# Four graph layers on one core: interleaved bn_stats without merging, probability copies on VectorE, and new orders of work

## The chip, the cores and the metric

The kernel runs on one core of a Trainium2 chip. Its time is the device time in microseconds, from one launch, median of three runs. In the core, TensorE (PE), VectorE (DVE), ScalarE (ACT), GpSimd (POOL) and SyncE (SP) each work through their own list of instructions and wait for each other by semaphores. Here SP issues all transfers of the steady state.

## The reference

128 graphs of 128 nodes with 256 features pass through four residual layers over one adjacency matrix. Each begins with a layer norm and a ReLU:

```
def _layernorm(x, axis=-1, eps=1e-05):
    m = jnp.mean(x, axis=axis, keepdims=True)
    v = jnp.var(x, axis=axis, keepdims=True)
    return (x - m) / jnp.sqrt(v + eps)
...
    h = jnp.maximum(_layernorm(x, axis=-1), 0.0)
    x = x + _L0_gnn_ref(h, adj, L0_gnn_W, L0_gnn_a)        # graph attention, 128 features, and the features themselves
    h = jnp.maximum(_layernorm(x, axis=-1), 0.0)
    x = x + _L1_gnn_ref(h, adj, L1_gnn_W, L1_gnn_b)        # deg * (x Wi + b) + A (x Wj)
    h = jnp.maximum(_layernorm(x, axis=-1), 0.0)
    x = x + _L2_gnn_ref(h, adj, ...)                       # masked attention, 8 heads of 32
    h = jnp.maximum(_layernorm(x, axis=-1), 0.0)
    x = x + _L3_gnn_ref(h, adj, L3_gnn_W, L3_gnn_a_src, L3_gnn_a_dst)   # graph attention, 256 features
```

## The kernel before

Two graphs (GROUP = 2) make a group, and 64 groups pass through a pipeline of eight parts, 0 to 7. Every engine has a function `slot` that lists its pieces in a fixed order, each with its part: `at(5, split_head_3)` does that piece for group t - 5. `run` calls `slot` for t = 0 to 70 (64 groups and PARTS = 7). One pass over the list is called a slot in this text. The order inside a slot is written out by hand for each engine, and a piece waits by semaphore for the piece that feeds it and for the one that frees its PSUM bank.

The eight PSUM banks of 512 fp32 columns are shared by name: `f0_ps`, `sc0_ps` and so on each point to a bank. x of a group lies as `[128 nodes, 2 graphs, 256]` in fp32, in one of 11 buffers.

A layer goes like this. VectorE takes the statistics of x, one bn_stats for each graph (six numbers: count, mean and summed squares of the even and of the odd elements), and one bn_aggr for each graph merges them to mean and variance. GpSimd makes the scale and shift from them (`add_eps`, `negate_mean`, `power`, `shift`). ScalarE applies them with the ReLU (`norm0_0`, `norm0_1`, one for each graph). GpSimd splits the result into a high and a low fp16 part (`rows_hi`, `rows_lo`), SP transposes both by DMA (`move0` to `move3`), and TensorE multiplies by weights that are split in the same way, three matmuls for one product (`triple`). The two attention layers with one head (0 and 3) turn the probabilities on TensorE (`turn_probs0`, `turn_probs3`). ScalarE copies them from PSUM to SBUF (`keep_probs0`, `keep_probs3`), TensorE sums with them (`gat_sum0`, `gat_sum3`) and VectorE adds the result to x (`update0_0`, `update3_0` and their partners). The head attention keeps its probabilities in PSUM, casts them on ScalarE (`keep_head`), subtracts on VectorE (`split_head`) and turns both parts by DMA (`move_heads_hi`, `move_heads_lo`).

A slot has on TensorE: 90 matmuls of 256 or 258 columns (84 of the weights' triples, four for biases, two for masks), 12 of 130 columns, 48 of 33 columns, two of 512 for the gather, four fp32 ones each of 256 and 129 columns as recorded, eight small fp32 ones of 128, and the head scores. On SP it has one load of x, seven transposes and one store.

Of the kernel before, what the change touches and what calls it, by code (L numbers as in the profile page):

```python
# [21 lines left out]
FOLD = [0, 1, 2, 3]  # L22
# [20 lines left out]
def build(nc, x_in, adj, adj_t, w0, w0_t, a0, w_i, w_j, b1, w_q, w_k, b_qk, w_v, b_v, w_o, b_o, w3, w3_t, a3, out):  # L43
# [7 lines left out]
    with ctx:  # L51
# [42 lines left out]
        stats0 = pair("stats0", [P, GROUP, 6], F32)  # L94
        moments0 = pair("moments0", [P, GROUP, 2], F32)
        vareps0, rstd0, nmean0, nshift0 = (pair(n, [P, GROUP], F32) for n in ("vareps0", "rstd0", "nmean0", "nshift0"))
        relu0 = pair("relu0", [P, GROUP, D], F32)
        stats1 = pair("stats1", [P, GROUP, 6], F32)
        moments1 = pair("moments1", [P, GROUP, 2], F32)
        vareps1, rstd1, nmean1, nshift1 = (pair(n, [P, GROUP], F32) for n in ("vareps1", "rstd1", "nmean1", "nshift1"))  # L100
        relu1 = pair("relu1", [P, GROUP, D], F32)
        stats2 = pair("stats2", [P, GROUP, 6], F32)
        moments2 = pair("moments2", [P, GROUP, 2], F32)
        vareps2, rstd2, nmean2, nshift2 = (pair(n, [P, GROUP], F32) for n in ("vareps2", "rstd2", "nmean2", "nshift2"))
        relu2 = pair("relu2", [P, GROUP, D], F32)
        stats3 = pair("stats3", [P, GROUP, 6], F32)
        moments3 = pair("moments3", [P, GROUP, 2], F32)
# [45 lines left out]
        f0_ps = ps[6]  # L153
        r0_ps = ps[6]
        p0_ps = ps[0]
        s0_ps = ps[0]
        mj_ps = ps[5]
        mi_ps = ps[2]
        ag_ps = ps[5]
        q_ps = ps[0]  # L160
        k_ps = ps[4]
        v_ps = ps[5]
        sc0_ps = ps[7]
        sc1_ps = ps[4]
        sc2_ps = ps[1]
        sc3_ps = ps[3]
        sh0_ps = ps[0]
        sh1_ps = ps[2]
        pr_ps = ps[2]
        f30_ps = ps[7]  # L170
        f31_ps = ps[3]
        r3_ps = ps[5]
        p3_ps = ps[6]
        s3_ps = ps[6]
# [16 lines left out]
        stats0_0_done = sem("stats0_0_done")  # L191
# [4 lines left out]
        norm0_1_done = sem("norm0_1_done")  # L196
# [14 lines left out]
        update0_0_done = sem("update0_0_done")  # L211
        update0_1_done = sem("update0_1_done")
        add_feat0_done = sem("add_feat0_done")
        stats1_1_done = sem("stats1_1_done")
# [6 lines left out]
        relu_lo1_done = sem("relu_lo1_done")  # L221
        move1_done = [sem(f"move1_done_{k}") for k in range(2)]
# [7 lines left out]
        stats2_1_done = sem("stats2_1_done")  # L230
# [4 lines left out]
        norm2_0_done = sem("norm2_0_done")  # L235
# [7 lines left out]
        split_query_done = sem("split_query_done")  # L243
# [5 lines left out]
        head_max_0_done = sem("head_max_0_done")  # L249
        head_exp_0_done = sem("head_exp_0_done")  # L250
        head_max_1_done = sem("head_max_1_done")
# [4 lines left out]
        keep_head_0_done = sem("keep_head_0_done")  # L256
# [4 lines left out]
        split_head_2_done = sem("split_head_2_done")  # L261
# [17 lines left out]
        stats3_1_done = sem("stats3_1_done")  # L279
# [12 lines left out]
        leaky3_0_done = sem("leaky3_0_done")  # L292
# [3 lines left out]
        inv_sum3_done = sem("inv_sum3_done")  # L296
# [3 lines left out]
        update3_1_done = sem("update3_1_done")  # L300
# [12 lines left out]
        def _(sp):  # L313
# [51 lines left out]
            def move_heads_lo(g):  # L365
                sp.wait_ge(split_head_2_done, g + 1)
                sp.dma_start(head_t_lo[g % 2][:, :, :], head_lo[g % 2][:, :, :].rearrange("p a n -> p (a n)"), transpose=True).then_inc(move_heads_lo_done[g % 2], 16)
# [9 lines left out]
            def store_x(g):  # L377
                sp.wait_ge(update3_1_done, g + 1)
                sp.dma_start(out_groups[g], x[g % XBUF][:, :, :]).then_inc(x_moved[g % XBUF], 16)

            def slot(at):
                at(0, load_x)
                at(7, move3)
                at(6, move_out)
                at(2, move1)
                at(5, move_heads_hi)
                at(5, move_heads_lo)
                at(0, move0)
# [8 lines left out]
        def _(pe):  # L397
# [41 lines left out]
            def feat0(g):  # L439
# [3 lines left out]
                if g >= 7:  # L443
                    pe.wait_ge(update3_1_done, g - 6)
# [6 lines left out]
            def logit_rows0(g):  # L451
                if g == 0:
                    pe.wait_ge(mask_ready, 1)
                pe.wait_ge(keep_feat0_done, g + 1)
                logit_rows(r0_ps, g0[g % 2], 130).then_inc(logit_rows0_done, 1)

            def turn_probs0_0(g):
                pe.wait_ge(expo0_0_done, g + 1)
                if g >= 3:
                    pe.wait_ge(split_query_done, g - 2)  # L460
# [12 lines left out]
            def message_source(g):  # L473
# [3 lines left out]
                if g >= 5:  # L477
                    pe.wait_ge(leaky3_0_done, g - 4)
# [6 lines left out]
            def message_own(g):  # L485
                if g == 0:
                    pe.wait_ge(w_split, W_TURN.index("i") + 1)
                if g >= 4:
                    pe.wait_ge(update2_done, g - 3)
# [12 lines left out]
            def make_query(g):  # L502
# [4 lines left out]
                if g >= 2:  # L507
                    pe.wait_ge(split_out_0_done, g - 1)
# [9 lines left out]
            def make_key(g):  # L518
                if g == 0:
                    pe.wait_ge(w_split, W_TURN.index("k") + 1)  # L520
                if g >= 1:
                    pe.wait_ge(split_head_1_done, g)
# [433 lines left out]
        def _(act):  # L956
# [16 lines left out]
            def norm0_1(g):  # L973
# [4 lines left out]
                if g == 0:  # L978
                    hi_part("i", COL_WI, D)
# [359 lines left out]
```

## Time and profile before

| | us |
|---|---|
| median of three runs | 1150.78 (1149.5 to 1151.24) |
| time of the profiled execution | 1155.16 |
| its span, first to last instruction | 1153.4 |
| PE busy | 1067.4 (93%) |
| DVE busy | 1045.6 (91%) |
| ACT busy | 1057.2 (92%) |
| POOL busy | 950.6 (82%) |

The mean granted TensorE clock is 0.978 of full speed. Busy time is the time in which at least one instruction of an engine is shown. Instructions overlap in it, since the next one starts before the last has written its result, so what an instruction costs its engine is the distance from its start to the next start where nothing is waited for. The shares hold the fill and the drain of the pipeline too; between them all four engines are busier.

### The profile page before, as it was taken

Reading aid. Unit: us, or ns where it says so; the run is one execution under the profiler, and the core shown is the slowest. Engines: PE = TensorE matmul, PEld = TensorE weight load, DVE = VectorE, ACT = ScalarE, POOL = GpSimd, SP = SyncE. Lnnn points to the kernel's source line nnn. Section 1 sums busy time; section 2 is a strip of 40 time slices with the busy share of each in tenths; the row PEclk is TensorE's granted clock in tenths of the full one; section 3 lists DMA queues with packets and bytes.
Section 4 is the critical chain, followed back from the end, with each engine's and each line's share of the span. In section 5 each row is a group of like instructions: output and inputs, shape, how many; then the busy total and the mean of one; then the engine's idle time right before and its main releaser. Section 6 shows DMA issues by size and latency. Waiting matters only on the chain.

```text
span 1153.4 us, 38860 instructions
## 1 busy us (share of the span) xinstructions
PE 1067.4 (93%) x14872; PEld 881.4 (76%) x14872; DVE 1045.6 (91%) x2911; ACT 1057.2 (92%) x3145; POOL 950.6 (82%) x1734
## 2 busy tenths in 40 slices
PE   4589999999999999999999999999999999999864
PEld 3467888888888878788878878887888888888642
DVE  4469999999999999999999999999999999999861
ACT  3479999999999999999999999999999999999852
POOL 3778998998988889898989889888988899898421
PEclk9889999999999999999999999999999999999985
DMA  5369999999999999999999999999999999999861
GB/s 148 65 110 147 180 175 172 187 184 172 175 184 175 164 177 182 170 183 172 175 180 174 177 182 171 172 184 184 167 175 184 178 182 168 183 179 156 140 121 40
DMA packets 643515, 190.07 MB, mean 165 GB/s; under 512 B 607232, under 2 KB 643328, under 8 KB 643328
## 3 DMA queue, kind: packets, MB, share of 16 engines
q1 hardware_dynamic: 642560, 187.24, 93.6%
q8 instruction: 118, 1.93, 0.7%
q14 instruction: 69, 0.57, 0.2%
q10 hardware_dynamic: 768, 0.33, 0.1%
HBM read 19.73 MB, written 16.78 MB: 32 GB/s over the span
## 4 chain that ended last, share of the span: by engine, by line
ACT 32%; DVE 32%; DMA 16%; PE 11%; issue 3%; POOL 3%; SPq 1%; DVEq 0%; POOLq 0%
DMA x<-in_x 9%; DMA h_t<-h_rows 5%; DMA mix_t<-mix_rows 3%; PE ps L406 3%; PE ps L408 2%; PE ps L407 2%; DVE x L787 2%; DVE head_nmax L826 2%; ACT ps L1060 2%; DVE head_nmax L822 2%; DVE x L878 2%; ACT ps L1055 2%; ACT ps L1049 2%; ACT ps L1066 2%; ACT relu L971 1%
## 5 line engine op out<-in xcount | busy, mean ns | idle before, releaser
L406 PE MATMUL ps<-w_hi,h_t 128*128 128x256 f16 (+2 forms) x1280 | 328.3, 266 | 31.1 <-DMA h_t<-h_rows 21.5
L407 PE MATMUL ps<-w_lo,h_t 128*128 128x256 f16 (+2 forms) x1280 | 329.9, 265 | 0.0
L408 PE MATMUL ps<-w_hi,h_t 128*128 128x256 f16 (+2 forms) x1280 | 329.7, 265 | 0.0
L406 PEld LDWEIGHTS ps<-w_hi,h_t 128*128 128x128 f16 x1280 | 125.4, 98 | 59.3 <-DMA h_t<-h_rows 26.9
L408 PE MATMUL ps<-h_t,w_lo 128*128 128x256 f16 x512 | 139.6, 273 | 0.0
L407 PE MATMUL ps<-h_t,w_hi 128*128 128x256 f16 x512 | 139.6, 273 | 0.0
L406 PE MATMUL ps<-h_t,w_hi 128*128 128x256 f16 x512 | 139.6, 273 | 0.0
L408 PEld LDWEIGHTS ps<-w_hi,h_t 128*128 128x128 f16 x1280 | 125.8, 98 | 14.3
L407 PEld LDWEIGHTS ps<-w_lo,h_t 128*128 128x128 f16 x1280 | 126.5, 99 | 12.4
L406 PEld LDWEIGHTS ps<-v_hi,head_t_hi 128*128 128x128 f16 x1024 | 82.5, 96 | 13.5 <-issue 4.2
L406 PE MATMUL ps<-v_hi,head_t_hi 128*128 128x33 f16 x1024 | 90.4, 178 | 1.3 <-issue 1.2
L407 PEld LDWEIGHTS ps<-v_lo,head_t_hi 128*128 128x128 f16 x1024 | 80.1, 96 | 13.5 <-issue 0.6
L408 PE MATMUL ps<-v_hi,head_t_lo 128*128 128x33 f16 x1024 | 90.4, 178 | 0.0
L407 PE MATMUL ps<-v_lo,head_t_hi 128*128 128x33 f16 x1024 | 90.3, 178 | 0.0
L1227 POOL TENSOR_TENSOR x<-x,deg_b 128x512 f32<-128x512 f32 x64 | 81.7, 1276 | 0.0
L1247 POOL TENSOR_TENSOR x<-x,out_bias 128x512 f32<-128x512 f32 x64 | 81.2, 1269 | 0.0
L408 PEld LDWEIGHTS ps<-v_hi,head_t_lo 128*128 128x128 f16 x1024 | 79.9, 96 | 0.0
L1222 POOL TENSOR_TENSOR h_rows<-relu,h_rows 128x512 f16<-128x512 f32 x64 | 73.9, 1155 | 5.3
L1060 ACT ACTIVATE ps<-ps,head_nmax 128x128 f32<-128x128 f32 x256 | 77.3, 448 | 0.0
L1278 POOL TENSOR_TENSOR h_rows<-relu,h_rows 128x512 f16<-128x512 f32 x64 | 74.3, 1161 | 0.4
L1255 POOL TENSOR_TENSOR h_rows<-relu,h_rows 128x512 f16<-128x512 f32 x64 | 74.1, 1158 | 0.3
L1195 POOL TENSOR_TENSOR h_rows<-relu,h_rows 128x512 f16<-128x512 f32 x64 | 74.0, 1157 | 0.3
(181 smaller groups left out, 4445.4 us busy)
## 6 DMA issues: line engine op xcount, KB each, us to landing
x<-in_x SPq DMA_DIRECT2D x64, 256.0 KB, 3.3
out<-x SPq DMA_DIRECT2D x64, 256.0 KB, 2.6
h_t<-h_rows SPq DMA_TRANSPOSE x256, 3.8
head_t_hi<-head_hi SPq DMA_TRANSPOSE x64, 4.5
head_t_lo<-head_lo SPq DMA_TRANSPOSE x64, 6.1
mix_t<-mix_rows SPq DMA_TRANSPOSE x64, 3.5
w_f<-in_w_o SPq DMA_DIRECT2D x1, 256.0 KB, 3.8
w3t_f<-in_w_t SPq DMA_DIRECT2D x1, 256.0 KB, 3.8
```

The lines of the kernel that those rows point to most:

```text
L406: pe.matmul(o, lh, rh, start=start, stop=False)
L407: pe.matmul(o, lh, rl, start=False, stop=False)
L408: return pe.matmul(o, ll, rh, start=False, stop=stop)
L787: dve.scalar_tensor_tensor(x[g % XBUF][:, :, :], mi_ps[:, :].rearrange("p (b n) -> p b n", b=GROUP), deg_unscale[:, 0:1], x[g % XBUF][:, : ...
L822: dve.tensor_reduce(head_nmax[g % 2][:, 0, :], sc0_ps[:, :].rearrange("p (j n) -> p j n", n=P), AX.X, ALU.max, negate=True).then_inc(head_ ...
L1060: last = act.activation(sc2_ps[:, j * P:(j + 1) * P], sc2_ps[:, j * P:(j + 1) * P], ACT.Exp, bias=head_nmax[g % 2][:, 2, j:j + 1])
L1195: pool.tensor_tensor(h0_rows[g % 2][:, 1, :, :], relu0[g % 2][:, :, :], h0_rows[g % 2][:, 0, :, :], ALU.subtract).then_inc(rows_lo0_done, 1)
L1222: pool.tensor_tensor(h1_rows[g % 2][:, 1, :, :], relu1[g % 2][:, :, :], h1_rows[g % 2][:, 0, :, :], ALU.subtract).then_inc(relu_lo1_done, 1)
L1227: pool.tensor_tensor(x[g % XBUF][:, :, :], x[g % XBUF][:, :, :], deg_b1[:, :].unsqueeze(1).to_broadcast([P, GROUP, D]), ALU.add)
L1247: pool.tensor_tensor(x[g % XBUF][:, :, :], x[g % XBUF][:, :, :], out_bias[:, :].unsqueeze(1).to_broadcast([P, GROUP, D]), ALU.add)
L1255: pool.tensor_tensor(h2_rows[g % 2][:, 1, :, :], relu2[g % 2][:, :, :], h2_rows[g % 2][:, 0, :, :], ALU.subtract).then_inc(rows_lo2_done, 1)
L1278: pool.tensor_tensor(h3_rows[g % 2][:, 1, :, :], relu3[g % 2][:, :, :], h3_rows[g % 2][:, 0, :, :], ALU.subtract).then_inc(rows_lo3_done, 1)
```

## The change

Three things are changed. First, each layer takes the statistics of both graphs by one bn_stats over 512 elements: the access pattern `p b n -> p n b` makes graph 0 the even and graph 1 the odd elements, so that the six numbers are count, mean and summed squares of the one and the other. The bn_aggr go, and GpSimd takes the mean at index 1 and the sum at index 2, which it scales by 1/256. Second, `keep_probs0` and `keep_probs3` move from ScalarE to VectorE. Third, every engine has a new order of its slot, PSUM banks are dealt out anew, and semaphores follow both. The number of parts, of buffers and of transfers is as it was.

```
-            def stats3_0(g):
+            def mean_var3(g):
                 dve.wait_ge(update2_done, g + 1)
-                dve.bn_stats(stats3[g % 2][:, 0, :], x[g % XBUF][:, 0, :])
-
-            def stats3_1(g):
-                dve.bn_stats(stats3[g % 2][:, 1, :], x[g % XBUF][:, 1, :]).then_inc(stats3_1_done, 1)
-
-            def mean_var3(g):
-                dve.wait_ge(stats3_1_done, g + 1)
-                dve.bn_aggr(moments3[g % 2][:, 0, :], stats3[g % 2][:, 0, :])
-                dve.bn_aggr(moments3[g % 2][:, 1, :], stats3[g % 2][:, 1, :]).then_inc(mean_var3_done, 1)
+                dve.bn_stats(stats3[g % 2][:, :, :].rearrange("p b s -> p (b s)"), x[g % XBUF][:, :, :].rearrange("p b n -> p n b")).then_inc(mean_var3_done, 1)
...
-                pool.tensor_scalar(vareps3[g % 2][:, :], moments3[g % 2][:, :, 1], 1.0, EPS, ALU.mult, ALU.add).then_inc(add_eps3_done, 1)
+                pool.tensor_scalar(vareps3[g % 2][:, :], stats3[g % 2][:, :, 2], 1.0 / D, EPS, ALU.mult, ALU.add).then_inc(add_eps3_done, 1)
...
-            def keep_probs3(g):
-                act.wait_ge(turn_probs3_1_done, g + 1)
-                act.activation(prob_t3[g % 2][:, :], p3_ps[:, 0:GROUP * P], ACT.Copy).then_inc(keep_probs3_done, 1)
...
+            def keep_probs3(g):
+                dve.wait_ge(turn_probs3_1_done, g + 1)
+                dve.tensor_copy(prob_t3[g % 2][:, :], p3_ps[:, 0:GROUP * P]).then_inc(keep_probs3_done, 1)
```

The other three layers' statistics and `keep_probs0` change alike. SP's new order:

```
                 at(0, load_x)
+                at(1, move0)
                 at(7, move3)
                 at(6, move_out)
-                at(2, move1)
                 at(5, move_heads_hi)
                 at(5, move_heads_lo)
-                at(0, move0)
+                at(2, move1)
                 at(3, move2)
                 at(7, store_x)
```

The new orders of the other engines, in short form (part, piece), as they stand after the change:

```
vector: 2 mean_var1, 6 head_norm_1, 5 split_head_3, 5 head_max_2, 6 split_out_0, 3 split_message, 6 split_out_1,
  3 update1_own, 0 mean_var0, 3 update1, 3 mean_var2, 5 split_head_1, 5 split_head_2, 5 split_head_0,
  4 split_query, 4 split_key, 1 row_max0, 6 update2, 6 mean_var3, 7 row_max3, 4 head_max_0, 1 keep_probs0,
  4 head_max_1, 7 inv_sum3, 7 keep_probs3, 4 head_max_3, 4 split_value, 1 inv_sum0, 7 update3_1, 7 update3_0,
  1 update0_0, 5 invert_heads_0, 1 update0_1, 5 head_norm_0, 5 invert_heads_1
scalar: 3 norm2_0, 3 norm2_1, 1 expo0_0, 1 expo0_1, 7 leaky3_0, 7 leaky3_1, 0 norm0_1, 7 expo3_0, 7 expo3_1,
  0 norm0_0, 4 keep_value, 6 norm3_0, 6 norm3_1, 4 head_exp_3, 4 head_exp_1, 4 keep_head_3, 5 keep_out_0,
  4 head_exp_0, 2 keep_message, 5 keep_out_1, 4 keep_head_1, 4 head_exp_2, 4 keep_head_0, 4 keep_head_2,
  0 keep_feat0, 1 norm1_1, 1 norm1_0, 3 cast_query, 0 leaky0_1, 3 cast_key, 6 keep_feat3_1, 0 leaky0_0,
  6 keep_feat3_0
tensor: 1 turn_probs0_1, 4 make_value, 7 turn_probs3_0, 7 turn_probs3_1, 1 gat_sum0, 7 gat_sum3, 5 head_sum_0,
  5 head_sum_1, 2 message_source, 2 message_own, 3 make_query, 2 gather, 0 feat0, 3 make_key, 0 logit_rows0,
  6 feat3_1, 6 feat3_0, 5 project_0, 5 project_1, 6 logit_rows3, 3 head_scores, 0 turn_probs0_0
```

## Rows read from the trace of the kernel before

**Rows 1.** The page, part 1: busy time, share of the span and instructions.

```profile
PE 1067.4 (93%) x14872; PEld 881.4 (76%) x14872; DVE 1045.6 (91%) x2911; ACT 1057.2 (92%) x3145; POOL 950.6 (82%) x1734
```

**Rows 2.** Windows, steady stretch: busy time (instructions), clock, DMA share, GB/s.

```profile
200.00:1000.00 800.00, 781.55 (x11230) 653.10 (x11227) 777.36 (x2179) 790.90 (x2373) 716.61 (x1303) 1.00 1.02 177
```

**Rows 3.** Timeline, DVE, one slot: start, length, engine, line, operation.

```profile
599.38 0.68 DVE L829 TENSOR_REDUCE head_nmax<-ps 128x4 f32<-128x512 f32 x1
...
601.56 0.68 DVE L840 TENSOR_TENSOR head_lo<-ps,head_hi 128x512 f16<-128x512 f32 x1
603.05 0.43 DVE L729 BATCH_NORM_STATS2 stats<-x 128x6 f32<-128x256 f32 x1 [0.80 <-DMA x<-in_x]
...
603.72 0.41 DVE L801 BATCH_NORM_STATS2 stats<-x 128x6 f32<-128x256 f32 x1
604.04 0.17 DVE L733 BATCH_NORM_AGGREGATE moments<-stats 128x2 f32<-128x6 f32 x1
...
604.33 0.39 DVE L742 TENSOR_REDUCE nmax<-leaky 128x2 f32<-128x256 f32 x1
...
616.27 0.68 DVE L829 TENSOR_REDUCE head_nmax<-ps 128x4 f32<-128x512 f32 x1
```

**Rows 4.** Timeline, ACT, the same slot.

```profile
603.47 0.77 ACT L1036 ACTIVATE query_hi<-ps 128x512 f16<-128x512 f32 x1
604.75 0.40 ACT L998 ACTIVATE prob<-leaky,nmax 128x128 f32<-128x128 f32 x1 [0.51 <-DVE nmax L742]
...
608.39 0.38 ACT L1007 ACTIVATE prob_t<-ps 128x256 f32<-128x256 f32 x1
608.65 0.61 ACT L1032 ACTIVATE relu<-x,nshift,rstd 128x256 f32<-128x256 f32 x1
```

**Rows 5.** Timeline, PE, around the sum of layer 3.

```profile
612.66 0.27 PE L408 MATMUL ps<-w_hi,h_t 128*128 128x256 f16 x1
612.77 1.03 PE L636 MATMUL ps<-g,prob_t 128*128 128x256 f32 x4
613.64 0.18 PE L406 MATMUL ps<-v_hi,head_t_hi 128*128 128x33 f16 x1
613.67 0.18 PE L407 MATMUL ps<-v_lo,head_t_hi 128*128 128x33 f16 x1
```

**Rows 6.** Waits from 200 to 1000: total us, times, longest.

```profile
DVE stats L729 <- DMA x<-in_x: 12.2, 19, 1.2
```

**Rows 7.** Timeline, DVE: neighbours that wait for nothing but each other.

```profile
607.02 0.68 DVE L814 SCALAR_TENSOR_TENSOR key_lo<-ps,key_hi 128x512 f16<-128x512 f32 x1
607.62 0.68 DVE L878 SCALAR_TENSOR_TENSOR x<-ps,x 128x512 f32<-128x512 f32 x1
608.34 0.43 DVE L882 BATCH_NORM_STATS2 stats<-x 128x6 f32<-128x256 f32 x1
...
616.87 0.41 DVE L870 TENSOR_TENSOR mix_rows<-ps,mix_rows 128x256 f16<-128x256 f32 x1
617.20 0.41 DVE L874 TENSOR_TENSOR mix_rows<-ps,mix_rows 128x256 f16<-128x256 f32 x1
```

**Rows 8.** Timeline, SP and DVE: last update, load of x, first statistics.

```profile
614.56 0.43 DVE L907 SCALAR_TENSOR_TENSOR x<-ps,inv,x 128x256 f32<-128x256 f32 x1
...
615.46 0.48 SPq L318 DMA_DIRECT2D x<-in_x  x1
...
619.05 0.41 DVE L729 BATCH_NORM_STATS2 stats<-x 128x6 f32<-128x256 f32 x1
```

**Rows 9.** Timeline, all engines, the last group in the drain.

```profile
1144.88 0.36 ACT L1108 ACTIVATE leaky<-ps,g 128x128 f32<-128x128 f32 x1
1145.27 0.42 DVE L894 TENSOR_REDUCE nmax<-leaky 128x2 f32<-128x256 f32 x1 [8.51 <-ACT leaky L1108]
1145.73 0.40 ACT L1116 ACTIVATE prob<-leaky,nmax 128x128 f32<-128x128 f32 x1 [0.49 <-DVE nmax L894]
...
1147.17 0.38 ACT L1125 ACTIVATE prob_t<-ps 128x256 f32<-128x256 f32 x1 [0.56 <-PE ps L631]
```

More of the change, by code:

```diff
@@ L910, in slot @@
             def slot(at):
-                at(6, head_norm_0)
+                at(2, mean_var1)
                 at(6, head_norm_1)
+                at(5, split_head_3)
                 at(5, head_max_2)
                 at(6, split_out_0)
+                at(3, split_message)
                 at(6, split_out_1)
-                at(3, stats2_0)
-                at(5, split_head_3)
+                at(3, update1_own)
+                at(0, mean_var0)
+                at(3, update1)
+                at(3, mean_var2)
@@ L932, in slot @@
-                at(6, stats3_1)
+                at(6, mean_var3)
                 at(7, row_max3)
-                at(6, mean_var3)
+                at(4, head_max_0)
+                at(1, keep_probs0)
                 at(4, head_max_1)
+                at(7, inv_sum3)
+                at(7, keep_probs3)
+                at(4, head_max_3)
+                at(4, split_value)
                 at(1, inv_sum0)
-                at(4, head_max_3)
+                at(7, update3_1)
+                at(7, update3_0)
@@ L938, in slot @@
                 at(1, update0_0)
-                at(7, inv_sum3)
+                at(5, invert_heads_0)
                 at(1, update0_1)
-                at(1, stats1_0)
-                at(1, stats1_1)
-                at(4, head_max_0)
-                at(1, mean_var1)
-                at(2, split_message)
-                at(2, update1_own)
-                at(7, update3_0)
-                at(5, invert_heads_0)
-                at(7, update3_1)
-                at(2, update1)
+                at(5, head_norm_0)
@@ L979, in norm0_1 @@
                     hi_part("i", COL_WI, D)
+            def norm0_1(g):
+                act.wait_ge(shift0_done, g + 1)
+                act.activation(relu0[g % 2][:, 1, :], x[g % XBUF][:, 1, :], ACT.Relu, bias=nshift0[g % 2][:, 1:2], scale=rstd0[g % 2][:, 1:2])
             def keep_feat0(g):
@@ L1160, in slot @@
+                at(5, keep_out_0)
+                at(4, head_exp_0)
                 at(2, keep_message)
-                at(7, keep_probs3)
-                at(6, norm3_0)
+                at(5, keep_out_1)
+                at(4, keep_head_1)
+                at(4, head_exp_2)
+                at(4, keep_head_0)
+                at(4, keep_head_2)
+                at(0, keep_feat0)
+                at(1, norm1_1)
+                at(1, norm1_0)
+                at(3, cast_query)
+                at(0, leaky0_1)
```

354 lines of the change are left out of this document (149 added, 205 removed).

## The prediction

> **What bounds the kernel now.** I read the windows first. In the 800 us from 200 to 1000, tensor, vector and scalar are busy 781.55, 777.36 and 790.90 us, GpSimd 716.61 [rows 2]. Vector runs 45 instructions per group (2911 in all, about 30 of them for the setup) [rows 1], so the 2179 of that stretch are 48.4 slots, and a slot takes 800 / 48.4 = 16.52 us. Nobody is far from full; the question is who is full by need and who by waiting.
>
> For that the timeline of one vector slot is read by the distance from one start to the next, since the durations overlap (0.68 us for an operation that is followed after 0.60). From `head_max_3` to `head_max_3` it is 616.27 - 599.38 = 16.89 us. `split_head_1` at 601.56 is followed only at 603.05 by the statistics that wait for x, 1.49 us in place of 0.60: 0.89 us of waiting [rows 3]. Some 0.1 us more stands before `head_max_1`. What is left, **15.9 us, is vector's work per slot**. On scalar the same is done at the step from `cast_query` to `expo0_0`: 604.75 - 603.47 = 1.28 us where 0.48 would do, and little elsewhere, so **scalar's work is about 15.95 us** of those 16.89 [rows 4]. (The number is my estimate: 16.89 less 0.80 less about 0.1.)
>
> Tensor looks 97.7% busy, but a matmul that is shown for 0.27 us is followed after 0.11, a fp32 one of 256 columns after about 0.22, one of 33 columns after 0.025 [rows 5]. Each break in the stream therefore adds a tail that costs nothing. By these spacings I estimate a slot's work: 90 matmuls of 256 columns or about that 9.9 us, 12 of 130 columns 0.7, 48 of 33 columns 1.2, the fp32 sums and turns 2.2, the gather 0.4, the head scores about 1.1, together 15.4 us. GpSimd: 716.61 / 48.4 = 14.8.
>
> So two engines with 15.9 us each, in a slot of 16.52: 0.6 us is lost as they wait for each other, for x and for tensor. The chain of waits over the same stretch names x as the largest of vector's: 12.2 us, 0.25 per slot [rows 6].
>
> **The change, part by part.**
>
> *Statistics.* Removed per slot: eight bn_stats over 256 elements and eight bn_aggr. Two of the first take 603.72 - 603.05 = 0.67 us, so 0.33 each, 2.65 for eight. The last of three starts at 603.72 and the first merge at 604.04; four merges fill 604.04 to 604.33, 0.07 each, 0.58 for eight with the two that stand behind another operation at 0.09 [rows 3]. That is 3.23 us off vector. Added: four bn_stats over 512 elements, which alternate between the two graphs' rows, 1 KB apart. No row reads SBUF in such steps. If the stream runs at full rate, the price is that of 256 more elements on 0.33: operations over 512 elements follow each other after 0.60 [rows 7], so 0.33 + 0.27 = 0.60, and four cost 2.40. That is the lower bound. The upper bound is every element read at half rate: 0.60 + 0.53 = 1.13, four cost 4.52. I take 0.60, because it is what the vector operation of 512 elements costs in these rows, and bn_stats over 256 lies on the same line as the others of 256 (0.33).
>
> The Trainium skill speaks against this in one place: "Advanced Engine Details and Errata", section "Memory Cachelines", says that an access to a different 16-byte line each time pays a penalty. Its "Vector Engine (DVE) Microarchitecture Reference", section 5.2, gives 1.73 ns per column for a two-source operation of which one source hops at every element, yet says that a one-source operation alternating between two regions was measured at full rate. No run here shows either. By 1.73 ns the operation would cost an estimated 0.95 us, vector 17.2 us per slot, and the kernel about 1205 us.
>
> *A new neighbour.* `mean_var2` now stands right behind `update1`, whose result it reads. Where that is so today, `update2` before the statistics, the step is 608.34 - 607.62 = 0.72 instead of 0.60 [rows 7]: plus 0.11.
>
> *Copies of turned probabilities.* `keep_probs0` and `keep_probs3` leave scalar. `keep_probs0` is followed after 608.65 - 608.39 = 0.26 us [rows 4]; two of them are 0.53 off. On vector an operation of 256 columns from PSUM costs 617.20 - 616.87 = 0.33 [rows 7], two 0.66 more.
>
> *Sum.* Vector 15.9 - 3.23 + 2.40 + 0.11 + 0.66 = 15.84 us. Scalar 15.95 - 0.53 = 15.42. Tensor 15.4 and GpSimd 14.8 as before; the smaller inputs of `add_eps` and the scale 1/D cost nothing new. So vector alone bounds the slot, and its own work hardly shrinks: the gain has to come from waiting, 0.6 us today.
>
> *The orders.* On SP, the load of x stands behind the store as before; today the store's releaser `update3_1` starts at 614.56, the load is issued at 615.46 and its reader starts at 619.05, 4.5 us behind 614.56 [rows 8]. In the new order vector starts `update3_0` with about 1.4 us left in the slot (that operation, `update0_0`, `invert_heads_0`, `update0_1`, `head_norm_0`, `invert_heads_1`), and `mean_var0` comes after eight operations, 4.0 us: 5.4 us. 0.9 us more room covers the wait of 0.25. Moving `move0` behind the load and `move1` behind the two head moves changes when SP issues, not how often; the number of transposes (seven per slot) and the depth (PARTS, 7) stay, so I book the fill and drain at zero. With scalar 0.4 us below vector, its results should more often lie ready.
>
> I therefore take the wait from 0.6 to 0.3 us: slot 15.84 + 0.3 = 16.14, that is 0.38 less than 16.52; over 64 slots 24 us. Against the profiled span of 1153.4 (its own time was 1155.16) this is 1129; against the median of the runs, 1150.78, it is **1127 us**.
>
> **Rivals.**
>
> *Waits stay (1145).* Vector and tensor are then the pair that gets in each other's way, the DMA share stays at 1.02 [rows 2], and 0.6 us remain: 15.84 + 0.6 = 16.44, 0.08 x 64 = 5 us, 1145. For it: three engines within 0.5 us. Against it: the largest wait, for x, has a cause that the order removes.
>
> *The interleaved read is slow (1200).* It decides from where vector's work passes 16.52 less the 0.3 of waits, 16.22: 0.38 us over my sum, or 0.70 us per operation instead of 0.60. At the upper bound of 1.13 vector has 15.84 + 2.12 = 17.96, with 0.1 of waits (all others have slack) 18.06, 1.54 x 64 = 99 us, 1250. The middle between 1151 and 1250 is 1200. For it: a stream whose every element lies elsewhere is nowhere in the trace. Against it: the output is six numbers, and only one source is read.
>
> *The softmax of the last layer runs out of room on vector (1165).* The chain goes from `row_max3` over scalar and tensor to `keep_probs3`, now vector's, and on to `gat_sum3` and `update3_1`, in one slot. In the drain, where nobody else interferes, the first half takes 1147.17 - 1145.27 = 1.90 us [rows 9]; the new order leaves vector 0.32 + 0.60 + 0.33 + 0.60 + 0.07 = 1.92. The second half needs 0.38 for the copy, 1.03 for four matmuls [rows 5] and about 0.1 for two handovers, 1.5; the order leaves 0.33 + 0.60 + 0.60 + 0.10 = 1.63. Scalar too has only `norm0_1`, 0.49, between `leaky3_1` and `expo3_0`, where 1145.73 - 1144.88 = 0.85 from start to start is needed [rows 9], against 0.25 + 0.49: 0.11 lost, which its slack pays. If both halves miss by 0.3, tensor being late, the slot is 16.14 + 0.6 = 16.74, 0.22 x 64 = 14 us, 1165; it decides at 0.38 missed in all.
>
> **How the numbers follow.** Forecast 0.50, waits stay 0.20, slow read 0.20, no room 0.10. The forecast's own range goes from waits of nearly none (15.84 + 0.05, 0.63 x 64 = 40 us, 1110) to 1140. The whole range reaches over the waits that stay and the case without room to just past the middle of the slow read, 1210; left out are its upper half and something below, 1108. About 0.2% (2.3 us) is what a measurement can tell from no change. Faster: 0.50 and most of 0.20, 0.65. Same: 0.07. Slower: slow read, no room without its mildest part, 0.28.
>
> **What would show it.** In the profile after: bn_stats over 512 elements near 0.68 us shown (0.60 to the next start) if right, 1.0 or more if the read is slow. Vector above 98% busy, scalar near 95%. The wait for x gone from vector. `update3_1` waiting for `gat_sum3`, or scalar's `expo3_0` for `row_max3` by more than 0.2 us per slot, would speak for the last rival. A slot other than 15.9 to 16.3 us in steady state makes the prediction wrong, and a fill longer than today's would eat the gain without touching the slot.

## The result and the profile after

Twenty runs of each kernel side by side: before 1152.27 us, after **1159.63 us**, ratio 1.0059 with a 95% interval of 1.0043 to 1.0075. The change makes the kernel 0.6% slower; 1127 us was forecast. The profiled execution of the changed kernel took 1159.29 us, its span 1157.5. I read it in the order of the prediction. The page's busy line:

```profile
PE 1059.5 (92%) x14872; PEld 884.9 (76%) x14872; DVE 1049.1 (91%) x2271; ACT 1042.4 (90%) x3017; POOL 950.4 (82%) x1734
```

The windows of the steady stretch, columns as in [rows 2]:

```profile
200.00:1000.00 800.00, 773.05 (x11147) 652.33 (x11144) 773.38 (x1683) 775.21 (x2259) 710.73 (x1297) 1.00 1.02 175
```

Vector now runs 45 - 12 + 2 = 35 instructions a slot (each layer loses two bn_stats and two bn_aggr and gains one bn_stats, and the two copies come in), so 1683 of them are 48.1 slots, and a slot takes 800 / 48.1 = **16.64 us**. Before it was 16.52 [rows 2]. The difference, 0.12 x 64 = 8 us, is the measured loss of 7.4: the loss lies in the slot, not in fill or drain. Tensor, vector and scalar are all less busy than before, and none is full: no engine became the bound by its work alone.

Vector's timeline, one slot from `update2` (L844) to the next:

```profile
595.51 0.69 DVE L844 SCALAR_TENSOR_TENSOR x<-ps,x 128x512 f32<-128x512 f32 x1 [0.72 <-PE ps L396]
596.24 0.70 DVE L848 BATCH_NORM_STATS2 stats<-x 128x6 f32<-128x512 f32 x1
596.86 0.40 DVE L852 TENSOR_REDUCE nmax<-leaky 128x2 f32<-128x256 f32 x1
...
597.78 0.41 DVE L725 COPY prob_t<-ps 128x256 f32<-128x256 f32 x1
598.11 0.68 DVE L793 TENSOR_REDUCE head_nmax<-ps 128x4 f32<-128x512 f32 x1
598.71 0.15 DVE L856 RECIPROCAL inv<-sum 128x2 f32<-128x2 f32 x1
598.88 0.43 DVE L860 COPY prob_t<-ps 128x256 f32<-128x256 f32 x1
...
606.36 0.70 DVE L713 BATCH_NORM_STATS2 stats<-x 128x6 f32<-128x512 f32 x1
606.97 0.68 DVE L767 TENSOR_TENSOR x<-ps,x 128x512 f32<-128x512 f32 x1
607.68 0.70 DVE L773 BATCH_NORM_STATS2 stats<-x 128x6 f32<-128x512 f32 x1
...
611.28 0.41 DVE L721 TENSOR_REDUCE nmax<-leaky 128x2 f32<-128x256 f32 x1
612.02 0.69 DVE L844 SCALAR_TENSOR_TENSOR x<-ps,x 128x512 f32<-128x512 f32 x1 [0.32 <-PE ps L396]
```

The distances between starts give the prices. The interleaved bn_stats of 512 elements costs 606.97 - 606.36 = 0.61 us (0.62 at L848): full rate. The copy costs 598.11 - 597.78 = 0.33, and `mean_var2` stands 607.68 - 606.97 = 0.71 behind `update1`. All three are as forecast. The slot is 612.02 - 595.51 = 16.51 us; 0.41 of it is the wait ahead of `update2` (0.74 from L721 in place of 0.33) and 0.10 the handover to `keep_probs3` (0.17 from L856 in place of 0.07). So vector's work is close to 16.0, where the sum said 15.84. A mean slot thus holds **about 0.65 us of waiting** (16.64 - 16.0), where the forecast had 0.3. The slot shown is typical: the medians of all 35 steps between 200 and 1000 us, less these two waits, add up to 16.0. The same sum for the kernel before gives 15.9, as the prediction read it, and so 0.6 of waiting.

What the changed kernel waits for, from the waits between 200 and 1000 us (total us, times, longest):

```profile
PEld ps L394 <- DMA h_t<-h_rows: 44.7, 48, 2.0
PE ps L394 <- DMA h_t<-h_rows: 22.9, 35, 1.5
DVE x L844 <- PE ps L396: 19.4, 36, 0.7
...
DVE stats L713 <- DMA x<-in_x: 0.4, 2, 0.2
```

The wait for x, the only one that the prediction had traced, fell from 12.2 us [rows 6] to 0.4, by the reason given. In its place tensor waits in every slot for a transpose, and vector's `update2` for tensor. (PEld and PE are tensor's weight loads and its matmuls. Both wait at the same place, so their times overlap, and their sum is a measure of comparison and not time lost.) Which of the four transposes it is, the source line of `move0` (L333) tells, with who waited for it:

```profile
L333 SPq DMA_TRANSPOSE h_t<-h_rows x48: 1231/1357/3095, 200.9 to 983.8; - x48
...
  PEld ps L394: 44.0, 47
  PE ps L394: 22.5, 34
...
DMA to landing us min/median/max: 3.5/4.2/5.3
```

In the kernel before, the same question about its `move0` (L345) gives:

```profile
L345 SPq DMA_TRANSPOSE h_t<-h_rows x48: 1231/1446/2474, 212.1 to 988.5; - x48
...
  PEld ps L406: 0.5, 1
  PE ps L406: 0.4, 1
```

So nearly all of tensor's waiting for h_t, 66.5 of 67.6 us, is for `move0`, for which hardly anybody waited before (0.9). The kernel before was not free of such waits: by the same count its tensor waited 13.5 us for h_t, nearly all of it that of other layers, 26.6 for vector's `head_lo` and 18.8 for scalar's probabilities. What is new is one wait at one place in every slot. What it costs tensor is read in its stream, where the first matmul of `feat0` (L394) follows the last one of `gather` (L489):

```profile
605.91 0.38 PE L489 MATMUL ps<-mj_lo,agg 128*128 128x512 f16 x1
606.39 0.23 PE L394 MATMUL ps<-w_hi,h_t 128*128 128x130 f16 x1
```

That is 0.48 us here and 0.82 in the mean of all slots, where 0.21 would do: tensor stands still for 0.6 us a slot.

### The profile page after: what moved, and what is told of

Same layout as the page of the kernel before. It is cut to its first block, busy times and chain, and to the rows that moved or that the text cites. A ratio compares the mean times of both kernels' runs of the same rounds, so it can differ in the third digit from the quotient of the medians.

```text
span 1157.5 us, 38095 instructions
## 1 busy us (share of the span) xinstructions
PE 1059.5 (92%) x14872; PEld 884.9 (76%) x14872; DVE 1049.1 (91%) x2271; ACT 1042.4 (90%) x3017; POOL 950.4 (82%) x1734
## 4 chain that ended last, share of the span: by engine, by line
DVE 35%; PE 32%; DMA 23%; SPq 4%; issue 2%; ACT 2%; POOL 1%; DVEq 0%; ACTq 0%; POOLq 0%
DMA h_t<-h_rows 19%; PE ps L394 10%; PE ps L396 9%; PE ps L395 9%; DVE stats L848 3%; DVE x L844 3%; DVE v_lo L785 3%; DVE head_nmax L799 3%; DVE head_nmax L790 3%; DVE head_nmax L793 3%; DVE prob_t L860 2%; SPq L367 2%; DVE x L868 2%; DVE x L863 2%; DMA x<-in_x 2%
## 5 line engine op out<-in xcount | busy, mean ns | idle before, releaser
L394 PE MATMUL ps<-w_hi,h_t 128*128 128x256 f16 (+2 forms) x1280 | 331.2, 266 | 53.6 <-DMA h_t<-h_rows 53.2
L394 PEld LDWEIGHTS ps<-w_hi,h_t 128*128 128x128 f16 x1280 | 125.3, 98 | 94.9 <-DMA h_t<-h_rows 76.6
L394 PE MATMUL ps<-h_t,w_hi 128*128 128x256 f16 x512 | 139.7, 273 | 0.0
L395 PEld LDWEIGHTS ps<-w_lo,h_t 128*128 128x128 f16 x1280 | 126.4, 99 | 13.5
L394 PE MATMUL ps<-v_hi,head_t_hi 128*128 128x33 f16 x1024 | 84.1, 178 | 2.7 <-DMA head_t_lo<-head_lo 2.6
L394 PEld LDWEIGHTS ps<-v_hi,head_t_hi 128*128 128x128 f16 x1024 | 80.0, 96 | 6.6 <-issue 4.9
L396 PE MATMUL ps<-v_hi,head_t_lo 128*128 128x33 f16 x1024 | 84.1, 177 | 0.0
L395 PE MATMUL ps<-v_lo,head_t_hi 128*128 128x33 f16 x1024 | 84.1, 177 | 0.0
L624 PE MATMUL ps<-g,prob_t 128*128 128x256 f32 x256 | 74.2, 413 | 7.1 <-DVE prob_t L860 3.1
L1010 ACT ACTIVATE ps<-ps,head_nmax 128x128 f32<-128x128 f32 x256 | 79.9, 486 | 0.0
L844 DVE SCALAR_TENSOR_TENSOR x<-ps,x 128x512 f32<-128x512 f32 x64 | 44.2, 691 | 35.1 <-PE ps L396 34.7
L999 ACT ACTIVATE ps<-ps,head_nmax 128x128 f32<-128x128 f32 x256 | 75.9, 423 | 0.0
L1140 POOL TENSOR_TENSOR h_rows<-relu,h_rows 128x512 f16<-128x512 f32 x64 | 74.4, 1163 | 0.5
```

What stands on the lines that cost most here:

```text
L394: pe.matmul(o, lh, rh, start=start, stop=False)
L395: pe.matmul(o, lh, rl, start=False, stop=False)
L396: return pe.matmul(o, ll, rh, start=False, stop=stop)
L624: last = pe.matmul(s3_ps[:, b * D:(b + 1) * D], prob_t3[g % 2][:, b * P:(b + 1) * P], g3[g % 2][:, b, 0:D], start=True, stop=True)
L844: dve.scalar_tensor_tensor(x[g % XBUF][:, :, :], pr_ps[:, :].rearrange("p (b n) -> p b n", b=GROUP), UNSCALE, x[g % XBUF][:, :, :], ALU.mu ...
L999: last = act.activation(sc0_ps[:, j * P:(j + 1) * P], sc0_ps[:, j * P:(j + 1) * P], ACT.Exp, bias=head_nmax[g % 2][:, 0, j:j + 1])
```

## The experiments

Three parts were mixed in the change: statistics, copies, orders. The first runs take them apart, the later ones follow the wait for `move0`. Each number is a median with the ratio to the kernel before, run on the same chip. The groups of runs had different chips, on which the kernel before took 1152.3 to 1153.9 us, so kernels of different groups are compared by their ratios.

### Statistics alone, copies alone, both in the old orders

The statistics' edit to the kernel before is that of the diff, with `mean_var` where it stood. The copies' edit, in the old orders:

```
 vector  at(6, update2)
+vector  at(1, keep_probs0)
+vector  at(7, keep_probs3)    # ahead of head_max_0
-scalar  at(1, keep_probs0)
-scalar  at(7, keep_probs3)
```

> Old orders, scalar still copies the probabilities; each layer's two bn_stats and two bn_aggr become one interleaved bn_stats. It stands where the merge stood, so the first one also has three operations more of room before it needs x. Vector's work per slot falls from about 15.9 to about 15.1 us, scalar keeps about 15.9. Loop theory (in the changed kernel a chain through the first layer's transpose sets the slot, and the parts themselves are sound): scalar bounds here, the waits on vector for x are gone, slot 16.1 to 16.4, 1125 to 1147 us, faster than before by 0.5 to 2.5%. Rival (an interleaved read disturbs others, for instance GpSimd, so the part itself is what costs): same or slower, 1150 us or more, with longer GpSimd or scalar instructions in the profile.

Measured: 1149.16 us, 0.9976 (0.996 to 0.9991).

> Old orders and old statistics; only the two copies of turned probabilities move from scalar to vector. Vector's work 15.9 + 0.66 = 16.5 us, scalar 15.4. Both theories of the whole change agree that this is slower; the sizes differ. If vector's work plus some waiting sets the slot: 16.8 to 17.1 us, 1168 to 1190 us. If scalar's load was what made the others wait, so that vector then runs nearly without waits: 16.6, near 1157 us.

Measured: 1180.88 us, 1.0251 (1.0228 to 1.0274).

> Interleaved statistics and copies on vector, in the orders of before (each copy is put on vector where scalar did it in time). Vector's work about 15.75, scalar 15.4. Loop theory, by which the new orders cost the gain: slot 16.0 to 16.3, 1120 to 1140 us, clearly faster than the changed kernel (1160). Rival, by which the mix of work is to blame whatever the order: 1155 us or more.

Measured: 1169.87 us, 1.0151 (1.0126 to 1.0176).

The windows of the run with the statistics alone:

```profile
200.00:1000.00 800.00, 778.43 (x11197) 656.42 (x11196) 752.22 (x1597) 792.36 (x2371) 716.56 (x1308) 1.00 1.02 177
```

Vector has 33 instructions a slot here, so the slot is 800 / (1597 / 33) = 16.53 us, the same as before, though vector is busy 25 us less in the stretch: the time it gained turned into waiting. The gain of 0.24% is less than the theory said, but the rival is not borne out either: GpSimd is busy 14.8 us a slot in both, scalar 16.3 and 16.4, so the interleaved read slows neither. Scalar, busy 792 us of the 800, has as much work as before, and I take it for what sets the pace. The copies alone cost 29 us; they put 0.66 on a vector that was as full as scalar, and the slot becomes 800 / (2214 / 47) = 16.98. Both together cost 17.6 us, so the new orders are worth 10 us against the old ones with the same work (1159.6 and 1169.9). The second run came out as its first theory said. My expectation for the third, that the loss came from the orders, was wrong in sign. It does not follow that the orders are good, only that they are better for this division of the work than the old ones with the copies at the places chosen here.

### Does the amount of transposed data matter?

From the third group on only a quarter of the heads' probabilities is transposed, so the attention's sums use stale values. The edit is the same in both kernels:

```
+q = QUADS if g < 2 else 1
-sp.dma_start(head_t_hi[..][:, :, :], head_hi[..][:, :, :]..., transpose=True)
+sp.dma_start(head_t_hi[..][:, 0:q * GROUP * KC, :], head_hi[..][:, 0:q, :]..., transpose=True)    # lo alike
```

> The changed kernel, but from the third group on the two transposes of the head attention's probabilities move one quarter of their data (0.75 MB of 2.75 MB per slot is left out, so the head attention sums with stale values for the rest); instructions, waits and orders stay. First-transpose theory: the first transposes land in 3.1 to 3.3 us instead of 4.2, about 1 us off the loop, slot 16.0 to 16.3, 1115 to 1140 us. Theory that landing times that vary make the 0.6 us in every version: also faster, about as much, and the same in the kernel before (next run). Theory that transfers do not matter and the engines' lists do: within 0.4%, 1155 to 1165 us.

> The kernel before with the same cut of the head attention's two transposes to a quarter (stale values for the rest). Landing-time theory: the 0.6 us per slot of waiting shrinks to 0.2 or less here too, slot 16.1, 1123 to 1135 us. First-transpose theory: the old order has more room around its transposes, so it gains less than the changed kernel, 1140 to 1148 us. Transfers do not matter: 1149 to 1155 us.

Measured: 1160.57 us, 1.0061 (1.0046 to 1.0076), for the changed kernel and 1151.78, 0.9986 (0.9968 to 1.0004), for the one before. The DMA share between 200 and 1000 fell from 1.02 to 0.72 and 0.71, and the time did not move. A DMA share of one is no bound here. The first-transpose theory was not put to the test, since `move0` landed after a median of 3.9 us in place of 4.2 and not after the 3.1 to 3.3 that it assumed; tensor's wait for it stayed at 64.7 us.

### Tensor reads the late transpose later

```
 tensor
-at(0, feat0)
 at(3, make_key)
-at(0, logit_rows0)
+at(0, feat0)
 at(6, feat3_1)
+at(0, logit_rows0)
```

> The changed kernel, with one difference in the list of TensorE: make_key is done before feat0, and feat3_1 before logit_rows0, so that TensorE has 1.5 us of work while the first layer's transpose is on its way, and 1.5 us less lie between that transpose and update2. Loop theory: the 1.4 us per slot in which TensorE waits for that transpose fall to under 0.3, vector's wait at update2 (0.4 us per slot) goes, slot 16.1 to 16.4, 1122 to 1145 us. Rival (all engines nearly full, or the DMA queues full, waits only move): within 0.4% of the changed kernel, 1155 to 1165 us.

Measured: 1192.05 us, 1.0349 (1.0319 to 1.0378). From its waits:

```profile
POOL x L1144 <- ACT g L938: 59.9, 46, 2.3
ACT g L938 <- PE ps L396: 58.4, 46, 2.2
PEld ps L401 <- ACT g L1052: 31.6, 45, 0.8
```

Tensor's wait for h_t fell to 8 us, for `move0` to 2.7, and it cost more than it saved: `feat0` now starts later for certain, and `keep_feat0` (L938) on scalar, with `keep_feat3_0` (L1052) eight places behind it, became late in nearly every slot. Both the theory and the rival said faster or the same, and both were wrong. No other place of the reader was tried; the next runs bring the transpose forward instead.

### SP and GpSimd: bring the transpose forward

Three edits to the changed kernel, alone and together:

```
 sync, S: move0 ahead of the store        gpsimd, G                sync, L: load early
 at(0, load_x)                            at(1, rows_hi0)         -at(0, load_x)
-at(1, move0)                            -at(7, rows_hi3)         +at(-1, load_x)
 ...                                      at(1, rows_lo0)
 at(3, move2)                            +at(7, rows_hi3)
+at(0, move0)
 at(7, store_x)
```

> The changed kernel; on SP alone the first layer's transpose stands ahead of the store and of the next load instead of behind both. In the changed kernel it is issued 0.43 us on average after GpSimd finished its rows, because store and load are just then being issued. First-transpose theory (the way norm3_1, rows_hi3, rows_lo0, first transpose, feat0, keep_feat0 is longer than the room that scalar's list leaves for it, and it is closed to a loop by scalar's list): 0.4 us earlier, scalar's wait at keep_feat0 falls from 0.6 to about 0.3 us, slot 16.3 to 16.5, 1138 to 1150 us. Rival (a wait of about 0.6 us per slot belongs to every version, from transfers whose landing varies, whatever the order): unchanged within 0.3%, 1156 to 1163 us.

> The changed kernel; on GpSimd rows_lo0 stands before rows_hi3 (which waits for the last layer's norm), and on SP move0 before the store. The first transpose can start 0.8 us (0.58 of work, 0.2 of waiting) plus 0.4 us earlier, nothing else is done later than by 1.1 us on GpSimd. First-transpose theory: scalar's wait at keep_feat0 and TensorE's for the transpose (1.4 us per slot) nearly go, slot 16.0 to 16.3, 1115 to 1138 us. Rival: same as the changed kernel within 0.5%, 1154 to 1166 us; the waits move to other pieces.

Measured: S alone 1211.14 us, 1.0501 (1.0485 to 1.0517); S and G 1179.64, 1.0208 (1.0181 to 1.0234). Both far off what I expected. The waits of S alone show why:

```profile
DVE stats L713 <- DMA x<-in_x: 62.9, 45, 2.9
```

`move0`, and the store with the load behind it, now come after `rows_lo0`, so the load of x goes out later, and vector wants x in the same slot. There are 11 buffers of x, but the list issues each load only in the slot in which vector reads it. Edit L takes that link away:

> The changed kernel with move0 ahead of the store and the load in SP's list, rows_lo0 ahead of rows_hi3 in GpSimd's, and load_x set for the next group. Without the last edit the same orders took 2.1% longer than before, with 39.9 us of waiting for x on vector. Theory of the loop: that wait was the whole harm; with it gone and move0 issued about 0.4 us earlier a slot, the slot is 16.1 to 16.4: 1125 to 1145 us. Rival (other links, those of scalar and GpSimd behind the moved steps): 1160 to 1180 us, with tensor or scalar waiting for each other as in the run with make_key ahead of feat0.

> The changed kernel with load_x set for the next group and nothing else. Theory (the loop that sets its slot passes through the place of move0 behind the store and the load in SP's list, not through the load's landing, for which vector waits 0.4 us in 800): no difference from the changed kernel, 1156 to 1163 us. Rival (the early load alone is what made the kernel with the three edits fast): 1135 to 1145 us.

> The changed kernel with move0 ahead of the store and the load in SP's list, and load_x set for the next group; GpSimd's list is as in the changed kernel (rows_hi3 before rows_lo0). Theory: the 5.0% that the first of these edits cost alone was the late load, and is gone; what is left is that move0 goes out about 0.4 us earlier a slot, so 0.2 to 0.4 us of the 16.66 a slot go: 1135 to 1150 us, vector's x wait below 5 us in 800. Rival (move0 was released by rows_lo0 anyway, so only the edit on GpSimd's list counts): 1155 to 1165 us.

> The changed kernel with rows_lo0 ahead of rows_hi3 in GpSimd's list and load_x set for the next group; move0 keeps its place behind the store and the load in SP's list. Measured so far: early load alone 1160 us, early load and move0's place 1159 us, those two and this order 1137 us. Theory A (move0 is released by rows_lo0, which waited behind rows_hi3 for norm3_1; only GpSimd's order counts, SP's place nothing): 1135 to 1142 us. Theory B (move0 is held up by both: by rows_lo0's place and by the store and load ahead of it in SP's list, and both must go): 1150 to 1162 us, with tensor's waits for move0's landing above 30 us in 800.

> The changed kernel with rows_lo0 ahead of rows_hi3 in GpSimd's list and nothing else. Theory A (only GpSimd's order counts; the load was late only where move0 went ahead of it): 1135 to 1145 us. Theory B (both orders must go): 1150 to 1162 us, within 0.3% of the run with the early load beside it, since the load goes out before move0 here and vector hardly waits for it.

| edits to the changed kernel | us | ratio to before (95%) |
|---|---|---|
| none | 1159.63 | 1.0059 (1.0043 to 1.0075) |
| L | 1159.99 | 1.0043 (1.0021 to 1.0065) |
| G | 1159.46 | 1.0043 (1.0025 to 1.0062) |
| G, L | 1159.37 | 1.0059 (1.0038 to 1.008) |
| S, L | 1159.33 | 1.0055 (1.0035 to 1.0075) |
| S, G, L | **1137.35** | **0.9869 (0.9848 to 0.989)** |
| S | 1211.14 | 1.0501 (1.0485 to 1.0517) |
| S, G | 1179.64 | 1.0208 (1.0181 to 1.0234) |

With L, neither S nor G gives anything, and both together give 22 us. The expectation for S and L was wrong, and theory B of the last two runs was right. The timelines show how, read from the start of `update2`. First the changed kernel (L863 is `update3_0`, L1219 `rows_hi3`, L1140 `rows_lo0`, L367 the store, L306 the load, L333 `move0`, L363 `move3`):

```profile
595.51 0.69 DVE L844 SCALAR_TENSOR_TENSOR x<-ps,x 128x512 f32<-128x512 f32 x1 [0.72 <-PE ps L396]
...
600.32 0.62 POOL L1219 TENSOR_SCALAR h_rows<-relu 128x512 f16<-128x512 f32 x1 [0.21 <-ACT relu L1048]
600.90 1.16 POOL L1140 TENSOR_TENSOR h_rows<-relu,h_rows 128x512 f16<-128x512 f32 x1
600.93 0.47 DVE L863 SCALAR_TENSOR_TENSOR x<-ps,inv,x 128x256 f32<-128x256 f32 x1
601.43 0.39 SPq L367 DMA_DIRECT2D out<-x  x1
601.87 0.47 SPq L306 DMA_DIRECT2D x<-in_x  x1
602.38 1.23 SPq L333 DMA_TRANSPOSE h_t<-h_rows  x1
603.65 1.53 SPq L363 DMA_TRANSPOSE h_t<-h_rows  x1
```

With G and L, `rows_lo0` is ready early, but the store still waits for `update3_0`:

```profile
594.50 0.69 DVE L844 SCALAR_TENSOR_TENSOR x<-ps,x 128x512 f32<-128x512 f32 x1 [0.72 <-PE ps L396]
...
599.18 1.16 POOL L1140 TENSOR_TENSOR h_rows<-relu,h_rows 128x512 f16<-128x512 f32 x1
...
600.42 0.39 SPq L367 DMA_DIRECT2D out<-x  x1
...
601.36 1.23 SPq L333 DMA_TRANSPOSE h_t<-h_rows  x1
602.64 1.34 SPq L363 DMA_TRANSPOSE h_t<-h_rows  x1
```

With S and L, `move0` waits for `rows_lo0`, and what is now behind it waits too:

```profile
594.55 0.69 DVE L844 SCALAR_TENSOR_TENSOR x<-ps,x 128x512 f32<-128x512 f32 x1 [0.54 <-PE ps L396]
...
599.94 1.16 POOL L1140 TENSOR_TENSOR h_rows<-relu,h_rows 128x512 f16<-128x512 f32 x1
601.12 1.23 SPq L333 DMA_TRANSPOSE h_t<-h_rows  x1
602.40 0.58 SPq L367 DMA_DIRECT2D out<-x  x1
603.03 0.49 SPq L306 DMA_DIRECT2D x<-in_x  x1
603.56 1.24 SPq L363 DMA_TRANSPOSE h_t<-h_rows  x1
```

With all three:

```profile
601.16 0.69 DVE L844 SCALAR_TENSOR_TENSOR x<-ps,x 128x512 f32<-128x512 f32 x1 [0.68 <-PE ps L396]
...
605.84 1.16 POOL L1140 TENSOR_TENSOR h_rows<-relu,h_rows 128x512 f16<-128x512 f32 x1
...
607.02 1.23 SPq L333 DMA_TRANSPOSE h_t<-h_rows  x1
...
609.46 1.24 SPq L363 DMA_TRANSPOSE h_t<-h_rows  x1
```

Start to start from `update2`, `move0` and `move3` are issued after 6.87 and 8.14 us (changed), 6.86 and 8.14 (G, L), 6.57 and 9.01 (S, L), and 5.86 and 8.30 (S, G, L). `move0` is held up by two things in parallel: by the store and load ahead of it, which wait for `update3_0`, and by `rows_lo0`, which stood behind `rows_hi3`. G removes only the second, and the first holds. S removes the first, wins 0.30 for `move0`, and pushes `move3` back by 0.87, since SP works in order. The source lines of the S and L run say so: nobody waits for `move0` any more (0.9 us), but for `move3` (L363) tensor does:

```profile
  PEld ps L394: 25.0, 26
  PE ps L394: 17.7, 20
```

Only with both is `move0` a full microsecond earlier and `move3` almost where it was. The windows of that kernel:

```profile
200.00:1000.00 800.00, 788.34 (x11382) 667.25 (x11381) 787.91 (x1720) 789.88 (x2310) 728.12 (x1326) 1.00 1.06 180
```

1720 / 35 = 49.1 slots of **16.28 us**; the work is the same, so the wait is down to about 0.3 us, and tensor's waits for h_t fell from 67.6 to 18.9 us, and the step from `gather` to `feat0` from 0.82 to 0.22. Over all slots between 200 and 960 us the mean distances from `update2` to the issue of `move0` and of `move3` are 6.98 and 8.63 us in the changed kernel, 7.00 and 8.56 with G and L, 6.56 and 9.24 with S and L, 5.87 and 8.64 with all three: the slots shown are typical. That is the forecast's slot (16.14) but for the 0.15 by which vector's work is larger.

### The early load in the old orders, and the copies back on scalar

> The kernel before with nothing changed but load_x set for the next group. Its vector waited 12.2 us in 19 of the 48 slots between 200 and 1000 us for the load it had issued in the same slot, 0.25 us a slot. Theory of the loop (that wait is a link of the loop that sets the slot): 0.1 to 0.25 us a slot go, 1135 to 1145 us. Rival (another loop of nearly the same length stands behind it): no more than 0.2% from before, the wait shows up on another line.

> The kernel before with the interleaved statistics alone and load_x set for the next group. The statistics alone gave 0.24% and left 13.4 us of waiting for x in 800; the early load alone gave the kernel before 0.43%. Theory (scalar's 15.9 us and its own links bound both): 0.4 to 0.9% faster than before, 1142 to 1148 us, vector's busy time about 755 in 800. Rival (the wait for x hid the worth of the statistics): 1.3% or more faster, below 1138 us.

Measured: L on the kernel before 1148.0 us, 0.9957 (0.9939 to 0.9975); with the statistics too 1145.68, 0.9935 (0.9912 to 0.9958). The first is below what theory expected: of the 0.25 us of waiting for x per slot only 0.06 was won (slot 800 / (2187 / 45) = 16.46), while GpSimd's wait for scalar's relu grew from 20.8 to 32.0 us. The wait that the profile named was four times what its removal gave here. The second run came out as its theory said.

Then the copies go back to scalar, in the changed kernel and in two with edits. `update3_1` gets a wait of its own for `inv_sum3`:

```
-vector at(1, keep_probs0), at(7, keep_probs3)
 scalar at(0, norm0_1)
+scalar at(1, keep_probs0)
 ...
 scalar at(0, norm0_0)
+scalar at(7, keep_probs3)
```

> The changed kernel with both copies of the turned probabilities given back to scalar (the first behind norm0_1, the second behind norm0_0 in its list); statistics, banks and all other orders stay. Vector has 0.69 us a slot less (15.2), scalar 0.7 to 0.8 more (about 16.2). Theory of the loop (the slot is the loop update2, last layer's softmax and update3_0 on vector, then the store, the load and move0 on SP's list, then feat0 to project on tensor): the two copies leave vector's stretch between update2 and update3_0, the loop becomes up to 0.7 us shorter, and tensor's wait for move0's landing falls below a third of its 68 us; scalar then bounds with 16.2 to 16.4 a slot: 1130 to 1145 us. Rival (the waits are the list's, on whatever engine is fullest, about 0.6 to 0.7 over its work): 16.8 or more, 1160 to 1175 us.

> As the run with the copies given back to scalar, and load_x in SP's list set for the next group (one slot earlier for each group), so that no load is read in the slot in which it is issued. SP issues as much per slot as before. Theory of the loop: in the changed kernel the load waited for nothing that vector missed (its wait for x is 0.4 us in 800), so this adds nothing: within 0.3% of the run beside it. Rival (the load's landing is a hidden link): 0.1 to 0.3 us a slot faster than it, that is 7 to 20 us.

> The kernel with the three edits (move0 ahead of store and load, rows_lo0 ahead of rows_hi3, load one slot early: 1137 us) with both copies of the turned probabilities given back to scalar. Vector's work is 15.2 a slot, scalar's 16.0 (its least in the earlier run with the copies on scalar). Theory (with the loop through move0 out of the way the fullest engine's work plus 0.3 to 0.4 sets the slot): 16.3 to 16.5, 1140 to 1152 us: no faster than with the copies on vector. Rival (the copies lengthen vector's stretch in every version): 16.1 or less, below 1130 us.

Measured: alone 1174.73 us, 1.0179 (1.015 to 1.0207); with L 1172.8, 1.0177 (1.0159 to 1.0196); with S, G and L 1149.0, 0.9956 (0.994 to 0.9972). So in the new orders the copies on vector are faster than at these places on scalar, by 1.2% without the edits and 0.9% with them, the reverse of the old orders. My theory of the first of these runs, that they lengthen vector's stretch from `update2` to `update3_0` and so the loop, fell: tensor still waits 59 us for h_t, and 0.2 us a slot were lost (800 / (1569 / 33) = 16.83). The waits of the run name a place for it:

```profile
DVE v_lo L782 <- ACT v_hi L995: 26.0, 48, 0.5
```

In every slot vector's `split_value` waits about half a microsecond for scalar's `keep_value` (L995), in front of which `keep_probs3` was put; in the changed kernel it never waits. So the place of the copy in scalar's list may matter as much as the engine that makes it: another place was not tried, and that vector is the better engine for the copies is shown only against this one. The early load changed nothing here and the run with S, G and L came out at 1149.0, both as their theories said. That the three edits gain 2.2% here, with the copies elsewhere, and 1.9% there, supports `move0`'s issue as the cause of that part.

## Why the prediction was wrong

**The statistics' price: right.** 0.60 was forecast, 0.61 measured; the rival of a slow interleaved read, with its 1200 us, did not occur. The passages of the Trainium skill that the prediction names point opposite ways. The Trainium skill's remark in "Vector Engine (DVE) Microarchitecture Reference", section 5.2, that a one-source operation alternating between two regions was measured at full rate, agrees with this trace, 0.61 us for a bn_stats over rows 1 KB apart. The penalty that the Trainium skill gives in "Advanced Engine Details and Errata", section "Memory Cachelines", was not to be seen here.

**The copies, the new neighbour, the x wait: right.** 0.33 each, 0.71 in place of 0.72, and 0.4 us of waiting for x left.

**Vector's sum: 15.84 forecast, about 16.0 measured.** Small, and worth about 10 us of the 33 missed. Base and terms were right (15.9; 3.24 off, 2.42 on for the four bn_stats, 0.11, 0.67 for the copies, by the medians of the steps). What the sum lacked is spread over steps whose neighbour changed, `update3_1` for one at 0.40 in place of 0.35, and the sum had no term for those.

**The wait, "from 0.6 to 0.3 us": this is the step that failed.** It came out at about 0.65. Of the waits I followed only the one for x, then argued from engine sums that "with scalar 0.4 us below vector, its results should more often lie ready", and wrote that moving `move0` behind the load "changes when SP issues, not how often; ... so I book the fill and drain at zero". The fill was as booked; the steady slot was not. By the prediction's own sign it is wrong: the slot was to be 15.9 to 16.3 us and vector busy above 98%, and they were 16.64 and 96.7%. When SP issues was the point: `move0` went from a place where nobody waited for it (0.9 us) to one behind a store that waits for vector's `update3_0`, and tensor waited for it in 47 of 48 slots (66.5 us).

SP's place was not all of it. From the end of `rows_lo0` to the first matmul of `feat0` a mean 5.7 us passed in the kernel before, 0.20 of them ahead of the issue of `move0`. In the changed kernel it is 4.7, 0.44 ahead of the issue, and 0.6 of it is tensor's standstill, so the new lists leave 4.1. The landing takes a median of 4.1 and 4.2 from the issue. Of the 1.6 us of room that was lost, SP's list took 0.24; the rest lies in the places of `rows_lo0` on GpSimd and `feat0` on tensor. The prediction put a price on none of the three.

The run with S, G and L shows it from the other side: no work changed, the wait fell to about 0.3 us a slot, and 1137.35 us lie 10 from the forecast. In the runs that took the two holds off singly, G and L or S and L, the slot stayed at 16.7, so it is the two together, not SP's list alone as I first thought.

**The rivals.** "Waits stay" was nearest in kind, with 0.6 us, but in its 1145 us vector was full and the waits came from engine fullness; measured it was one wait with a place. "The softmax of the last layer runs out of room" named the right stretch of vector's list and the wrong wait in it: `keep_probs3` lost 0.1 us a slot by the row above, not 0.6. Its neighbour `update3_0` mattered, as the releaser of the store in front of `move0`.

**Why 0.6% slower, then.** Against the kernel before, vector's slot is 0.12 us longer. By the medians of its steps about 0.09 of that is work (15.91 and 16.00) and 0.03 is waiting (0.62 and 0.65): neither shrank. Against the forecast's 16.14 the slot is half a microsecond too long, about 0.16 by the work and 0.35 by the waiting. In the old orders the statistics alone gained 0.24%, the copies alone lost 2.5%, and the new orders won back 0.9% of the 1.5% that both cost. What they left on the table was 1.9%, which the three edits recover.

## What to carry to other kernels

When a change writes the order of an in-order DMA queue anew, take each transfer in turn: what its predecessor in the list waits for, when its own source is ready, when its first reader comes. A transfer behind a store is as late as the store's producer on another engine. Count on two holds of equal length: test them together, since either alone may show nothing, or move the harm to the transfer behind. And where many buffers exist, look whether the list ever issues a load ahead of its slot, before an order is judged.

## What was not expected of the hardware

A bn_stats over 512 elements whose neighbours in the stream lie 1 KB apart takes no longer than the other vector operations of 512 elements here: 0.61 us from start to start, where they take 0.60. And a transpose's landing time hardly follows the mean load of the DMA engines: `move0` lands after a median of 4.2 us in the changed kernel at a DMA share of 1.02, after 3.9 with the small head moves at 0.72, but after 3.2 with S and L, at 1.02 again. What is in flight at the moment of issue may decide; no run here isolates that.
